# Softmax denominators by two 128-query halves, with GpSimd adding the two key halves of the second

## What is computed

```python
scores = jnp.einsum('bhsd,bhtd->bhst', q, k) * SCALE
scores = SOFTCAP * jnp.tanh(scores / SOFTCAP)
i = jnp.arange(S)[:, None]
j = jnp.arange(S)[None, :]
mask = (j <= i) & (i - j < WINDOW)
scores = jnp.where(mask, scores, jnp.float32(-1e+30))
probs = jax.nn.softmax(scores, axis=-1)
attn = jnp.einsum('bhst,bhtd->bhsd', probs, v)
```

## Time and profile before

| | |
|---|---|
| median of three runs | 744.89 us (743.75 to 745.23) |
| the profiled execution | 744.2 us, span 742.5 us |
| TensorE matmul busy | 651.2 us, 88% of the span |
| TensorE weight load busy | 525.9 us, 71% |
| VectorE busy | 392.0 us, 53% |
| ScalarE busy | 291.1 us, 39% |
| GpSimd busy | 261.3 us, 35% |

### The profile page before, as it was taken

The page is one execution under the profiler, slowest core; times in us unless marked ns, Lnnn a source line. Parts: engine busy times, 40 slices in busy tenths (PEclk is TensorE's granted clock), DMA queues, the critical chain, the costliest instruction groups (busy, mean ns, idle before and its releaser), DMA issues.

```text
span 742.5 us, 13736 instructions
## 1 busy us (share of the span) xinstructions
PE 651.2 (88%) x5121; PEld 525.9 (71%) x5122; DVE 392.0 (53%) x889; ACT 291.1 (39%) x477; POOL 261.3 (35%) x256
## 2 busy tenths in 40 slices
PE   0215889999999999999699999999799999999991
PEld 0215778888888888887589899998566767667660
DVE  7774264747475747563546994223444443444430
ACT  8651555555555555555343223435112122121110
POOL 1630122222232223221341115857245455454531
PEclk9999999999999999999999999999999999999996
DMA  9600000101010101020315333442665555655542
GB/s 313 254 0 1 1 2 1 59 1 58 0 56 0 56 0 56 0 86 1 143 57 222 120 105 114 145 148 85 241 111 93 107 98 100 112 93 106 102 57 39
DMA packets 24353, 62.08 MB, mean 84 GB/s; under 512 B 3008, under 2 KB 7104, under 8 KB 22912
## 3 DMA queue, kind: packets, MB, share of 16 engines
q1 hardware_dynamic: 14912, 41.16, 15.4%
q0 software_dynamic: 8736, 20.45, 15.3%
q10 hardware_dynamic: 672, 0.03, 0.1%
HBM read 38.56 MB, written 23.07 MB: 83 GB/s over the span
## 4 chain that ended last, share of the span: by engine, by line
PE 56%; DMA 25%; DVE 7%; issue 4%; ACT 1%; POOL 0%; DVEq 0%; POOLq 0%
PE PS L1498 26%; DMA out_tokens<-yo,dest 25%; PE scores L1498 12%; PE scores L1750 5%; PE PS L1609 5%; PE scores L1595 3%; PE PS L1563 1%; PE PS L1552 1%; DVE rden L1172 1%; DVE xt_l L1151 1%; PE PS L1632 1%; DVE bn L1123 1%; DVE wgu_l L1443 1%; DVE T L1205 1%; PE PS L1780 1%
## 5 line engine op out<-in xcount | busy, mean ns | idle before, releaser
L1498 PE MATMUL scores<-xb,sw 128*128 128x256 f32 x768 | 99.1, 286 | 2.5 <-issue 2.5
L1498 PEld LDWEIGHTS scores<-xb,sw 128*128 128x128 f32 x768 | 96.5, 193 | 4.6 <-issue 2.9
L643 POOL DMA_INDIRECT out_tokens<-yo,dest x39 | 61.7, 1583 | 93.3 <-DMA out_tokens<-yo,dest 91.1
L563 POOL TENSOR_SCALAR_AFFINE_SELECT probs<-probs 128x512 f32<-128x512 f32 x64 | 42.8, 692 | 112.0 <-ACT probs L742 112.0
L1498 PE MATMUL PS<-xt_h,w_h 128*128 128x256 f32 x256 | 76.2, 298 | 5.0 <-DVE xt_l L1151 4.1
L891 ACT ACTIVATE es<-scores 128x256 f32<-128x256 f32 x39 | 14.9, 383 | 163.2 <-PE scores L1498 163.2
L1832 PE MATMUL scores<-wd_sb,ehT 128*128 x156 | 73.5, 593 | 1.0 <-DVE ehT L1458 1.0
L1498 PE MATMUL PS<-xt_l,w_h 128*128 128x256 f32 x256 | 73.2, 286 | 0.0
L1498 PE MATMUL PS<-xt_h,w_l 128*128 128x256 f32 x256 | 73.1, 285 | 0.0
L1498 PE MATMUL scores<-wgu_h,xgT_h 128*128 x156 | 65.3, 419 | 4.3 <-DVE xgT_l L1462 4.3
L739 ACT ACTIVATE probs<-scores 128x1536 f32<-128x1536 f32 x32 | 46.6, 1455 | 49.7 <-PE PS L1609 33.2
(11 more groups left out here) (283 smaller groups left out, 1386.5 us busy)
## 6 DMA issues: line engine op xcount, KB each, us to landing
wgu_l<-in_wgu SPq DMA_DIRECT2D x8, 1024.0 KB, 6.7
T<-in_x SPq DMA_DIRECT2D x8, 512.0 KB, 8.0
w_raw<-in_wqkvo SPq DMA_DIRECT2D x8, 512.0 KB, 10.3
x_rows<-x SPq DMA_DIRECT2D x8, 512.0 KB, 2.8
x_cols<-x2T SPq DMA_DIRECT2D x8, 512.0 KB, 2.6
xc<-x_cols SPq DMA_DIRECT2D x8, 512.0 KB, 3.6
out_tokens<-T SPq DMA_DIRECT2D x8, 512.0 KB, 7.4
wd_sb<-in_wd SPq DMA_DIRECT2D x8, 512.0 KB, 6.8
```

Source lines behind the costliest of these rows:

```text
L563: ins = pool.affine_select(out=t, in_=t, compare_op=ALU.is_ge, fill=0.0, base=0, pattern=[[0, HC], [1, P]], channel_multiplier=-1)
L643: pool.indirect_dma_start(out[:, :], bass.IndirectOffsetOnAxis(dest[:, t:t + 1], 0), yo[:, t % 3, :], None, compute_op=ALU.add).then_inc(y ...
L1498: ins = pe.matmul(out, lhs(k, a), rhs(k, b), start=m == 0, stop=m == len(products) - 1)
```

## The change

1. **Denominators.** The eight matmuls with `ones` become eight of 128 columns each: for the queries 0 to 127 the masked scores of the first key half alone, and for the queries 128 to 255 one matmul over `sums`, the two key halves already added. No accumulation is left in them.
2. **GpSimd adds.** Behind each mask, GpSimd waits for its own mask and adds the columns 128 to 255 and 256 to 383 of the four heads into `sums` (128 partitions x 512 columns), of which there are two. TensorE waits for it (`sum_ready`) between the values and the denominators.
3. **Room.** `sums` takes the memory of `x2`. The second norm now goes to `front` for batches 0 to 5, to the memory of `q_h` for batch 6 and to `sums` for batch 7. In the loop `affine(b + 2)` therefore waits for two more things, that the last `x2` is stored and that it is transposed; for batch 6 the norm waits for the last scores.

```diff
-        x2 = sb("x2", [P, TT * C], fp32, scope)
+        sums = sb("sums", [P, 2, HC, P], fp32, scope)
...
+        sums_flat = sums[:, :, :, :].rearrange("p a h s -> p (a h s)")
+        x2_at = {"first": front[:, :], "mid": front[:, :], "late": qf, "last": sums_flat}
...
+                pool.wait_ge(mask_done, 4 * b + c + 1)
+                pool.tensor_tensor(sums[:, c % 2, :, :], of_four(c)[:, :, P:2 * P], of_four(c)[:, :, 2 * P:3 * P],
+                                   ALU.add).then_inc(sum_ready, 1)
...
-            def second_normed(b, first):
-                if not first:
+            def second_normed(part, b):
+                if not (isinstance(b, int) and b == 0):
                     dve.wait_ge(x2_stored, 16 * b)
-                normed(x2, b, rstd2_ready).then_inc(x2_ready, 1)
+                if part == "late":
+                    dve.wait_ge(scores_full, 4 * B)
+                normed(x2_at[part], b, rstd2_ready).then_inc(x2_ready, 1)
...
                 if has_next:
+                    if has_back:
+                        dve.wait_ge(x2_stored, 16 * b)
+                        dve.wait_ge(*filled(part, "X2T1", b))
                     affine(b + 2)
...
-                for off, lhs in ((0, lambda h, tt: v[:, tt, h * D:(h + 1) * D]), (S, lambda h, tt: ones[:, 0:D])):
-                    for tt in range(TT):
-                        for j in range(HC):
-                            h = HC * c + j
-                            pr = of_four(c)[:, j, :]
-                            ins = pe.matmul(od_bank[j * D:(j + 1) * D, off + tt * P:off + S], lhs(h, tt),
-                                            pr[:, 0:S] if tt == 0 else pr[:, S:S + P], start=tt == 0, stop=tt == TT - 1,
-                                            skip_group_check=True)
+                for tt in range(TT):
+                    for j in range(HC):
+                        h = HC * c + j
+                        pr = of_four(c)[:, j, :]
+                        pe.matmul(od_bank[j * D:(j + 1) * D, tt * P:S], v[:, tt, h * D:(h + 1) * D],
+                                  pr[:, 0:S] if tt == 0 else pr[:, S:S + P], start=tt == 0, stop=tt == TT - 1,
+                                  skip_group_check=True)
+                pe.wait_ge(sum_ready, 4 * b + c + 1)
+                for half in range(2):
+                    for j in range(HC):
+                        terms = of_four(c)[:, j, 0:P] if half == 0 else sums[:, c % 2, j, :]
+                        ins = pe.matmul(od_bank[j * D:(j + 1) * D, S + half * P:S + (half + 1) * P], ones[:, 0:D],
+                                        terms, start=True, stop=True, skip_group_check=True)
                 ins.then_inc(pv_done, 1)
...
+                src = {"mid": "mid", "late": "mid", "last": "late", "tail": "last"}[part]
+                transposes(part, "X2T", x2_at[src], s)
```

More of the change, by code:

```diff
@@ L347, in layer_kernel @@
             sem("scores_full"), sem("tanh_done"), sem("exp_done"), sem("mask_done"))
-        pv_done, att_ready, att_h_done, att_l_done = (
-            sem("pv_done"), sem("att_ready"), sem("att_h_done"), sem("att_l_done"))
+        sum_ready, pv_done, att_ready, att_h_done, att_l_done = (
+            sem("sum_ready"), sem("pv_done"), sem("att_ready"), sem("att_h_done"), sem("att_l_done"))
         x2_stored, x2T_stored = sem("x2_stored"), sem("x2T_stored")
@@ L446, in _, with store_x2 @@
                 sp.dma_start(sw_raw[:, j, :], ws[:, j, :]).then_inc(shared_loaded, 16)
-            def store_x2(b):
+            def store_x2(part, b):
                 sp.wait_ge(x2_ready, b + 1)
                 sp.dma_start(x2_rows[bass.ds(b * S, S), :].rearrange("(t p) c -> p t c", p=P),
-                             x2[:, :].rearrange("p (t c) -> p t c", t=TT)).then_inc(x2_stored, 16)
+                             x2_at[part].rearrange("p (t c) -> p t c", t=TT)).then_inc(x2_stored, 16)
             def store_x2T(part, b, s):
@@ L457, in store_x2T @@
                 sp.dma_start(x2_cols[bass.ds(b * P, P), :], x2T[:, :]).then_inc(x2T_stored, 16)
-            store_x2(0)
+            store_x2("first", 0)
             with sp.Fori(1, B - 2) as b:
                 store_x2T("mid", b - 1, b)
-                store_x2(b)
+                store_x2("mid", b)
             store_x2T("late", B - 3, B - 2)
@@ L475, in _ @@
             load_tokens(0)
-            store_x2(B - 2)
+            store_x2("late", B - 2)
             store_x2T("last", B - 2, B - 1)
@@ L480, in _ @@
             sp.dma_start(sw_raw[:, 2, :], ws[:, 2, :]).then_inc(down_loaded, 16)
-            store_x2(B - 1)
+            store_x2("last", B - 1)
             store_x2T("tail", B - 1, B)
@@ L668, in _ @@
             na = CB * ACT_STATS
-            unread = [t[:, S * k:S * (k + 1)] for t in (front, x2T, x2, vf) for k in range(CB)]
+            unread = [t[:, S * k:S * (k + 1)] for t in (front, x2T, sums_flat, vf) for k in range(CB)]
             for b, k, c in cols:
@@ L1230, in step @@
             def step(part, b, has_front, has_back, has_next):
-                first = isinstance(b, int) and b == 0
                 if has_front:
@@ L1265, in step @@
                     normalise(b + 1, 1)
-                second_normed(b, first)
+                second_normed(part, b)
             affine(0)
@@ L1622, in gate_transposes @@
                 pe.wait_ge(x2_ready, b + 1)
-                transposes(part, "X2T", x2, s)
+                src = {"mid": "mid", "late": "mid", "last": "late", "tail": "last"}[part]
+                transposes(part, "X2T", x2_at[src], s)
             def gate_partial(part, s):
```

## The result

The changed kernel takes **739.8 us** (median of five runs, 738.46 to 740.53) against 743.96 us for the kernel before, run beside it (five runs, 742.79 to 745.23). The ratio is 0.993, with a 95% interval of 0.9912 to 0.9947. On another chip, later, it was 740.75 against 745.24 us, a ratio of 0.9941 (0.9928 to 0.9954). So the change makes the kernel about 0.6% to 0.7% faster; predicted were 740.5 us, 0.6% less.

The account below looks back on a forecast made before the run. TensorE's matmuls were taken to bound attention's loop, other engines the last step. From 744.2 us profiled, - 4.8 (23 groups) + 0.45 (last step) = 739.8; for the run median, 744.89 - 4.4 = 740.5 us, range 738.0 to 743.6.

Parts of the forecast that it names:

- What a group saves: Each value group on TensorE: shorter denominators turn 0.43 + 0.22 into 0.22 + 0.22 us, 0.21 us less.
- the wait costs: Rival: each TensorE wait for `sum_ready` holds back weight loads, 0.14 us a group, giving 743.9 us; chance 0.12.
- Which groups count: Attention's 32 value groups: 23 lie on the chain, three of four in each loop step, saving 4.8 us.
- the fourth group: Group (b + 1, 1) in each loop step: off the chain, its saving only lengthens TensorE's wait for `xt_low`.
- The price of the sum: GpSimd's addition of 512 columns: 1.29 us each, between 1.18 and 1.51, made 32 times.
- The sum is covered in the loop: GpSimd's additions in the loop delay nobody, the tightest product having 0.2 us to spare; costed at nothing.
- The shared buffer costs nothing: `affine` waiting for the second norm's store and transposes: the store lands 0.7 us before `affine` begins, so nothing.
- The last step: GpSimd has no cover: (7, 2) saves nothing and the piece gets 0.45 us longer (0.3 to 0.7).
- The predicted pause of nearly 3 us: Last step: TensorE's standstill before the shared part's matmuls, 2.49 us before the change, was to grow to nearly 3 us.
- VectorE is held: Rival: GpSimd's sums hold VectorE between output projection and `Q0`, up to 1.29 us at eight places, 750.8 us; chance 0.05.
- The clock: Rival: the last step's half-clock stretch moves or is spared (738.9 us), or one more comes (742.1); chance 0.10 for either.

Follow-up runs that it names:

- sums_old_denoms: The changed kernel with GpSimd's additions and TensorE's wait kept, but the old denominator matmuls put back: 746.62 us, ratio 1.002 to the kernel before.
- short_no_sum: The changed kernel without the additions and the wait, second key half left out of the denominators: 741.18 us, ratio 0.9956 to the kernel before.
- share_only: The changed kernel's buffers and added waits for the second norm, with old denominators and no sum: 744.73 us, ratio 0.9999 to the kernel before.
- stats_early: The changed kernel with the first half's second statistics moved ahead of the second projection's addition on VectorE: 736.58 us, ratio 0.9897 to the kernel before.
- xt_low_first: The changed kernel with `xt_low` moved ahead of the second statistics on VectorE: 741.56 us, ratio 0.9948 to the kernel before.
- sum_twice: The changed kernel with every GpSimd addition issued twice, one after the other: 743.51 us, ratio 0.9989 to the kernel before.

## Why the prediction was right

- **What a group saves.** Right: 1.44 to 1.23 us, and no gap at the wait for the sum. The rival "the wait costs" gave 0.14 us a group; the profile has 0.
- **Which groups count.** Right for the main stretch and in the reason for the loop. The main stretch should hold 22 of the 23, 4.72 us, and it lost 4.72. The wait for `xt_low` went from 0.6 to 0.8 us in five steps. The 23rd, (7, 3), gave less: from the end of the shared part's matmuls to its product it takes 5.08 us instead of 5.22, and VectorE's reciprocal there (366.02) now starts right behind VectorE's own work on the gate. What the prediction left open is whether the fourth group could be had: only with VectorE's order changed too, and then in part.
- **The price of the sum.** 1308 ns measured, 1290 taken from the line between two subtractions; the ends were 1.18 and 1.51.
- **The sum is covered in the loop.** Right, shown by sums_old_denoms (265.99 against 266.04 us) and short_no_sum (261.25 against 261.32). With the addition doubled the cover is gone and the products wait, 7.5 us in all.
- **The shared buffer costs nothing.** Right, shown by share_only. One reservation: with `xt_low` first, `affine` waited four times for the store, 2.1 us in all, with no loss of TensorE. The cover of 0.7 us is thin.
- **The last step.** The mechanism was right in the profiled execution. The product of (7, 2) is released by the low part of (7, 1) behind the sum; it starts 8.91 us after the addition of T instead of 8.34, and the work behind the pause follows 1.66 us later in both kernels. That is the whole 0.57 us, against 0.45 predicted; the difference is the mask of (7, 3), which took 1.48 us where the prediction had 1.36. Two things that it didn't foresee lie ahead of that product: `var_eps` takes 0.35 us beside the sum of (7, 2), so that the group of (7, 2) comes 5.16 us after the addition of T (354.23) instead of 4.98 (357.33), and the denominators at half clock take 0.82 instead of 0.44 us. They added nothing here, since the low part ended later still; without them VectorE would have waited longer than the 0.27 us. In the second profile of the change the clock ended last. So a total this near 0.45 us is in part luck. Against the 9.79 us estimated for short_no_sum the sum costs 0.78 us in this step, an estimate too. The predicted pause of nearly 3 us was 1.82 us long by the chain, because the denominators and transposes ahead of it ran at half clock (the transposes 1.90 us instead of 1.02) while its end stayed where GpSimd put it.
- **The rivals.** "VectorE is held" had 0.05 and a price of 10 us for `xt_low`. `xt_low` stayed at 672 to 692 ns, so it fell. Its evidence against the rival was thin, though: the subtraction at 243.61 ends at 244.35 and `xt_low` starts at 244.31, an overlap of 0.04 us. In the change the sum (242.41 to 243.72) lies over `xt_low` (from 242.99) for 0.7 us, and that settles it. But VectorE does get held, in `var_eps`, which the prediction didn't look at. The Trainium skill (SBUF — State Buffer, section "SBUF: two separate sides") lets whichever of the two engines starts first hold a shared port pair for its whole instruction, where VectorE's is in a two-port mode or reads two inputs from SBUF. No row shows in which mode `var_eps` runs; its 0.95 us in stats_early, which end with the sum, agree with such a lock. "The clock" did happen, both ways, in the profiled execution: the stretch in the last step moved off the matmuls of the shared part (4.53 to 3.10 us), and one more came at 78 us and took it back (3.06 to 4.56). That the two cancel is luck, and what the clock did in the runs without a profile isn't shown.

The sum of the prediction, -4.8 + 0.45 = -4.4 us, stands against 4.2 us between the medians, and 4.5 between the two spans.

## What to carry to other kernels

Where the chain leaves an engine and comes back, a shorter instruction on that engine saves nothing at that place, and it also eats the slack of the engine waited for: count the instances on the chain one by one before multiplying. When a wait is to be shortened by reordering, measure the whole chain of the engine that is waited for, not only the transfer that is late: in the changed kernel putting `xt_low` first gained nothing, putting it one statistics instruction earlier gained 3.9 us. Work for an idle engine is cheap in the loop, where others run ahead of their users, and dear in the last step, where nobody does.

## What the runs showed of the hardware

**GpSimd's additions and subtractions stop some of VectorE's instructions and not others.** `var_eps`, a `TENSOR_SCALAR` on 2 columns from SBUF to SBUF, over the whole run (least, median, largest ns), in short_no_sum (without the sums), in the change and in stats_early:

```profile
L1136 DVE TENSOR_SCALAR var_eps<-mean_var x16: 168/169/171, 62.4 to 378.5; 128x2 f32<-128x2 f32 x16
```

```profile
L1140 DVE TENSOR_SCALAR var_eps<-mean_var x16: 169/171/352, 62.2 to 377.9; 128x2 f32<-128x2 f32 x16
```

```profile
L1140 DVE TENSOR_SCALAR var_eps<-mean_var x16: 169/171/948, 62.2 to 373.8; 128x2 f32<-128x2 f32 x16
```

It isn't the sum alone. In the loop of stats_early `var_eps` takes 0.56 us five times, and there it ends (242.37) with GpSimd's low part (242.34):

```profile
241.81 0.56 DVE L1140 TENSOR_SCALAR var_eps<-mean_var 128x2 f32<-128x2 f32 x1
```

```profile
241.61 0.73 POOL L578 TENSOR_TENSOR att_l<-att,att_h 128x256 fp32r<-128x256 f32 x1
```

The reciprocals from PSUM that start beside a sum keep their 1.75 us, and `xt_low`, with one input in PSUM, its 678 ns.

**Masks beside a normalising pair** make it 1.77 us (`front L1145` at 246.70 in xt_low_first, the mask from 246.78) instead of 1.00 (at 244.40 in stats_early, where the mask comes at 245.04, when both are under way). This was there before the change; its cost depends on how the two engines' orders happen to meet, and so an edit on VectorE can gain or lose 0.4 us of VectorE's time in a step by it (1.38 us in the change, 1.77 in xt_low_first).

**Half-clock stretches move with the gaps.** In each of the profiled executions the last step holds one or more stretches in which TensorE's matmuls take up to twice as long, behind one of the two pauses in which it stands still (3.1 us ahead of the group of (7, 2) and 1.8 us ahead of the shared part, in the change). Over 350 to 372 us the granted clock was 0.92 before and after the change, 0.84 in share_only, sums_old_denoms and short_no_sum, and 0.69 in sum_twice. By it the last step of two kernels with the same work there differs by over a microsecond (10.00 us before, 11.27 in share_only), so that differences of half a microsecond in that step are read from single rows, never from the total.
